# Merge stage of a transformer layer: the routing of 64 token tiles in seven parts (4 and six times 10) in place of five (15, 14, 13, 11, 11)

## The reference

```
x      = layernorm(x + attention(x))                 # attention ends in "@ Wo.T + bo"
probs  = softmax(x @ Wr.T)                            # 8 experts
scores, experts = top_k(probs, 2);  scores /= scores.sum()
cap    = 2560                                         # 1.25 * (8192 * 2 / 8)
for e in range(8):                                    # in this order
    elig = (experts == e).any() & ~fallback
    pos  = cumsum(elig) - 1                           # over all tokens, in order
    kept, overflow = elig & (pos < cap), elig & (pos >= cap)
    y[kept]     += ffn(x[kept], W1[e], W2[e]) * score
    y[overflow]  = ffn(x, fw1, fw2);  fallback |= overflow
x = layernorm(x + y)
```

## Time and profile before

| what | value |
|---|---|
| median of 3 runs | 3617.78 us (3613.65 to 3622.28) |
| the profiled execution | 3615.08 us, its span 3613.2 us |
| busy in the span | PE 90%, DVE 60%, ACT 59%, POOL 36% |
| merge | from 2217.8 to 2556.4 us of the span |
| scatters in the merge | 128, in five batches |

### The profile page before, as it was taken

The page is one execution under the profiler, slowest core; times in us unless marked ns, Lnnn a source line. Parts: engine busy times, 40 slices in busy tenths (PEclk is TensorE's granted clock), DMA queues, the critical chain, the costliest instruction groups (busy, mean ns, idle before and its releaser), DMA issues. The chain is left out here.

```text
span 3613.2 us, 61901 instructions
## 1 busy us (share of the span) xinstructions
PE 3247.5 (90%) x20776; PEld 2099.3 (58%) x20776; DVE 2157.0 (60%) x5248; ACT 2126.2 (59%) x4147; POOL 1289.1 (36%) x1772
## 2 busy tenths in 40 slices
PE   7995999999999999999999997663599999999992
PEld 4553454545454454544545454553588888888882
DVE  5675988888888888888888883564111111111115
ACT  4553898889888898988989892110233222332231
POOL 3333444444444444444444440335222222222221
PEclk9997999999999999999999998775799999999996
DMA  6666123233232323323233324332466666666666
GB/s 201 212 215 187 49 67 84 66 88 79 62 76 65 91 68 82 78 63 90 62 83 71 77 48 139 129 113 80 163 212 209 201 199 210 212 199 204 202 206 208
DMA packets 287150, 465.08 MB, mean 129 GB/s; under 512 B 58626, under 2 KB 195716, under 8 KB 268162
## 3 DMA queue, kind: packets, MB, share of 16 engines
q1 hardware_dynamic: 250370, 409.69, 37.9%
q0 software_dynamic: 25728, 34.82, 4.5%
q10 hardware_dynamic: 10752, 16.78, 1.2%
HBM read 316.25 MB, written 144.45 MB: 128 GB/s over the span
## 5 line engine op out<-in xcount | busy, mean ns | idle before, releaser
L808 DVE CUSTOM_DVE_ANT_0 tot<-sc,gbias 128x1024 f32<-128x1024 f32 x1024 | 1239.0, 1210 | 20.2 <-PE sc L708 12.3
L671 POOL TENSOR_SCALAR gbias<-slab_a,gs 128x484 f32<-128x484 f32 x1024 | 681.2, 667 | 962.2 <-DVE negm L808 935.2
L860 ACT ACTIVATE probs<-tot,negm 128x640 f32<-128x640 f32 (+2 forms) x1024 | 766.0, 748 | 77.6 <-DVE negm L808 75.8
L708 PE MATMUL sc<-ks,qs 120*128 120x512 bf16 x2048 | 616.2, 382 | 68.7 <-DMA qs<-far_d 36.8
L1410 ACT ACTIVATE f_hid<-f_ph,f_w_up 128x256 f32<-128x256 f32 (+1 forms) x584 | 268.0, 459 | 678.2 <-PE f_ph L1369 673.2
L869 ACT ACTIVATE far_t<-fb 128x512 f32<-128x512 f32 (+1 forms) x1024 | 580.3, 567 | 101.3 <-PE fb L745 91.4
L820 DVE COPY near_t<-pb 128x256 f32<-128x256 f32 (+1 forms) x1024 | 397.8, 389 | 210.2 <-PE pb L729 203.3
L1369 PE MATMUL f_ph<-f_xt,f_w_up 128*128 128x256 f32 (+1 forms) x2336 | 485.5, 366 | 11.1 <-DMA f_w_up<-in_w_up 10.4
L879 ACT ACTIVATE near_t<-pa 128x256 f32<-128x256 f32 (+1 forms) x1024 | 447.8, 437 | 69.2 <-PE pa L720 54.6
L1381 PE MATMUL f_py<-f_w_down,f_hid 128*128 128x256 f32 x2176 | 481.6, 379 | 0.0
L720 PEld LDWEIGHTS pa<-ident,probs 128*128 128x128 f32 x2560 | 327.1, 140 | 239.7 <-issue 93.1
(11 more groups left out here) (184 smaller groups left out, 2986.9 us busy)
## 6 DMA issues: line engine op xcount, KB each, us to landing
f_w_down<-in_w_down SPq DMA_DIRECT2D x73, 1152.0 KB, 5.3
f_w_up<-in_w_up SPq DMA_DIRECT2D x73, 1028.0 KB, 7.8
xg_d<-fill SPq DMA_DIRECT2D x113, 260.0 KB, 2.6
ks<-k_d SPq DMA_DIRECT2D x192, 128.0 KB, 4.2
qs<-q_d SPq DMA_DIRECT2D x384, 64.0 KB
v_d<-vt SPq DMA_DIRECT2D x16, 1024.0 KB, 6.2
vs<-v_d SPq DMA_DIRECT2D x32, 512.0 KB, 4.2
rcb<-rc_d SPq DMA_DIRECT2D x64, 256.0 KB
```

The source lines that it names most:

```text
L671: pool.tensor_scalar(gbias[x % NG][:, SIDE:SIDE + BAND], slab[:, hh, :], gs[u % 2][:, i, hh:hh + 1], 1.0, ALU.mult, ALU.mult).then_inc(gbi ...
L708: mm = pe.matmul(sc[:, x % 2, c * 512:(c + 1) * 512], qs[u % 2][0:120, hh, i * P:(i + 1) * P], ks[u % 2][0:120, hh, c * 512:(c + 1) * 512] ...
L808: dve.tensor_tensor_reduce(tot[x % 2][:], sc[:, x % 2, :], gbias[x % NG][:, w:w + N], -1.0, 3.0e38, ALU.add, ALU.min, negm[h % 2][:, c:c + ...
L860: act.activation(probs[x % 2][:, 0:hi - lo], tot[x % 2][:, lo:hi], ACT.Exp, bias=negm[h % 2][:, c:c + 1], scale=-1.0).then_inc(near_done, 1)
```

## The change

One tuple:

```
-PARTS = (15, 14, 13, 11, 11)
+PARTS = (4, 10, 10, 10, 10, 10, 10)
```

## The result

The changed kernel takes 3635.3 us (median of 9 runs, 3630.4 to 3645.8), the kernel before 3619.8 us (median of 9, 3613.7 to 3625.2): a ratio of 1.0041, 95% interval 1.0030 to 1.0052. It is 15.5 us slower. The forecast of 3630 us was 12.2 over the median of before that was known then, 3617.8, and its sum 14.2 over the profiled execution.

A forecast was written before the change was run, and what follows sets the result against it. The VectorE and TensorE slot chain was taken to bound the merge until its last scatters. About 36 us more work, 20 less hold and 2.6 less scattering gave +14.2 on 3615.1, stated as 3630 us, range 3600 to 3655.

The forecast's parts named there:

- The sum's 14.2 us: Whole kernel: last batch starts 16.8 us later, 2.6 us less scattering behind it, added to the profiled 3615.1 us.
- What bounds the merge: Merge: the chain of 80 slots on VectorE and TensorE bounds it until the last batch, only then GpSimd's scatters.
- The work of two parts: Merge chain: two added parts bring 36 us of work, some 18 to 19 us each on VectorE.
- The hold: Merge: TensorE's answers reach VectorE late while scatters run; 76.5 us before, some 57 after, about 12 per full window.
- The first rival: Scatter batches: short ones escape the hold, some 3 us a window; faster from 5 us down; 3594 us, chance 0.13.
- part 0: Merge slots 11 to 20, four tiles: 33.9 us; 54.0 us from the merge's start to the first batch.
- Part 1: Merge slots 21 to 30, ten tiles, beside a batch of 8 scatters: 39.6 us, including 1.0 of hold.
- Part 3: One of the merge's parts in slots 31 to 60, beside 20 scatters: 50 us.
- Parts 2 and 4: Parts of the merge in slots 31 to 60, each beside 20 scatters: 50 us each.
- Rival 2: Merge: hold in proportion to scatters beside slots, 0.72 us each, 78 us after; 3651 us, chance 0.20.
- rival 3: Merge: added routing is hidden because TensorE bounds plain slots; only the shorter last part counts; 3612.5 us, chance 0.12.
- rival 4: Merge: the hold belongs to a part, not its scatters; 19.1 us each, 115 over six; 3687 us, chance 0.03.

The follow-up runs named there:

- late_seven: The changed kernel (seven parts) with all scatters held back until the last part's places are known; 3721.9 us, 1.0293 to the kernel before.
- after_again: The changed kernel, unchanged, measured again on another chip where the kernel before took 3547.5 us; 3586.3 us, ratio 1.0102.
- one_scatter: The kernel before with one scatter a tile in place of two; 3540.3 us, ratio 0.9785.
- four_parts: The kernel before with four longer parts of 24, 18, 12 and 10 tiles; 3623.1 us, ratio 1.0014.
- late_five: The kernel before (five parts) with all 128 scatters held back until the last part's places are known; 3689.4 us, ratio 1.0188.
- before_again: The kernel before, unchanged, measured and profiled again on another chip; 3547.5 us.
- paused: The kernel before with GpSimd waiting after every fourth tile of a part, except the last, until its scatters have landed; 3560.4 us, ratio 1.0042.

## Why the prediction was right

The forecast was 3630 us and the measured time is 3635.3. The sum's 14.2 us stand against 15.5 measured between the medians and 18.8 in the profiled merge; added to the median known then, it would have given 3632 and not 3630.

- **What bounds the merge:** right. The last batch starts when the chain of slots is done, and from there to the next stage's first load it is 30.3 us, before 32.8: the two scatters fewer.
- **The work of two parts, 36 us:** right. 35.3 from the two profiles with the hold taken off, 33.9 and 36.0 with no hold in it at all (late_seven, after_again).
- **The hold, from 76.5 to 57:** right within 6 us; 62.5, with 14 us in a full window where 11 to 15 were kept. The method (cut the observed holds at the new length of a batch) was sound because the hold depends on how long a run of scatters lasts. The first rival had the direction (short batches are held less) and not the size: 3 us a window were expected by it, and 14 were measured. Its threshold was off too: with the forecast 12.2 us over the median and 12 us of hold in each of four windows, the change would break even at about 9 us a window; at 5 it would be well ahead.
- **The pieces:** part 0 took 58.1 in place of 54.0. Its slots 13 to 17 took 2.4 to 6.2 us each, 19.6 in sum, where slots 24 to 28 before took 17.0, and slots 2 and 3 took 1.3 us more than before; neither is explained. Part 1 took 37.0 in place of 39.6, with no hold in the short batch. Part 3 took 53.8 in place of 50: the stretch at half clock lasted longer than I had kept. Parts 2 and 4 took 48.8 and 48.7, with more hold and less work than kept. These errors cancel in part, which is luck: the chain came out 4.5 us longer than the sum, 5.5 more of hold and 1 less of work.
- **Rival 2 (proportion)** is excluded by one_scatter and four_parts, **rival 3 (hidden work)** by late_seven, **rival 4 (hold per part)** by late_five. The rule of the Trainium skill (SBUF — State Buffer, Who interferes with whom), that DMA never contends with a compute engine, agrees with the profile of before_again, where no hold appears beside the same scatters. In the profile of before the measurement decides against what the rule lets one expect: with scatters beside slots 76.5 us of hold, in late_five without them none. Whether what is late there is a contention in the sense of that rule, no run shows.
- **What the prediction did not see:** its price holds where the hold is. Without it the same change costs 38.8 us, and the hold can't be read off the code. That the kernel before and the changed one were both measured where the hold is, is luck too: beside before_again the changed kernel took 3586.3 us, outside the stated range.

What stays open: what holds TensorE's answers. The runs show that it takes scatters beside slots, that the first wait begins 9 to 20 us into an unpaused batch, that the second wait is the longer one in most batches, that the last ends 0.1 to 6.3 us after the batch's last scatter, and that pauses cut it down. By the times of the kernel before, it is there in every run of three comparisons and in none of two others. Whether it is the number of scatters, their bytes or GpSimd's issuing of them, no run here tells. Nor is it shown that the chip decides: no chip is on record in two comparisons, so a lasting difference between chips and something of the occasion can't be told apart.

## What to carry to other kernels

A chain that alternates between two engines pays for every further round: here two more parts cost 34 to 36 us whether or not scatters ran beside them. Count the rounds before making parts smaller. Where such a chain waits during long runs of indirect scatters, short pauses in the run are worth a try, checked on more than one chip: here one pause pattern gained 1.4% on one and cost 0.3% and 0.4% on two others. And compare only with runs of the kernel before on the same chip; by the absolute times alone, paused would have passed for a success on a chip where it was a loss.

## What the runs showed of the hardware

- The same kernel, before, takes 3620 us (medians 3619.8, 3622.3 and 3619.9 in three comparisons) or 3546 us (3545.8 and 3547.5 in two), without a single run between 3560.2 and 3606.7. The 74 us lie in the merge, where the hold is: 338.6 us against 264.9 for that stage, with 76.5 us of hold and none.
- Where the hold is, VectorE learned of a count 11 us after TensorE's 0.6 us for it began, beside indirect scatters issued every 1.28 us. Batches of 10 us had no such wait, batches of 26 us 13.5 to 15.1 us of them, and one of 61 us 54.
- Waiting for the landings, 2.5 to 4 us after every eighth scatter, left 22.5 us of hold in place of 76.5.
